# A graph network on one core: the columns of its dense count matrices, from one window's own to one per node

## The chip, the cores and the metric

The kernel runs on one core of one Trainium2 chip. The metric is device time in microseconds for one execution, as the median of repeated runs.

## The reference

Four graph layers run one after the other on 6250 nodes of 128 features and 100,000 edges. The edges are sorted by `dst`; `src` is random. `dst` is the square of a uniform number times 6250, so low nodes have many edges and high nodes few.

```python
x = _layernorm(x + tensor_product_layer(x, src, dst, edge_attr_4, edge_attr_10))
x = _layernorm(x + gated_gru_layer(x, edge_index))       # messages * sigmoid(att)
x = _layernorm(x + two_sort_convolutions(x, edge_index)) # 4 first edges of a node
x = _layernorm(x + four_sage_layers(x, edge_index))
# in a sage layer
msg = z[src]
agg = segment_sum(msg, dst, num_segments=n_nodes)
mean = agg / maximum(cnt, 1.0)
return mean @ Wl.T + bl + z @ Wr.T
```

Hidden widths of the sage layers are 256 after the first three and 128 after the last; inputs of the second to fourth are 256 wide.

## The kernel before, in words

**Tiles and groups.** 128 edges are a tile (784 tiles) and four tiles a group (196 groups). Everywhere but in the dense part a group is worked off thus: POOL issues an indirect gather of 128 rows for each tile, DVE makes one-hots of the edges' nodes relative to the group's base node, PE multiplies rows by one-hots into 128 columns of PSUM, and DVE adds those into the SBUF aggregate at the base, which it loads into a register.

**The dense part.** The first tiles, whose nodes have the most edges, are not gathered in the gate pass and the sage passes ("hot" tiles; the rest are "cold"). Instead a matrix holds, for each of 49 blocks of 128 source nodes and each column of the destination, how many edges run between them (f16, in HBM, `dense`). A pass then reads 49 blocks of counts and of the node table in order ("dense steps") and PE multiplies table by counts. Consecutive hot tiles, at most 16, form a window; a window has columns of its own, 16 to 34 of them, whose first stands for the window's first node. A node that two windows share has a column in each. The start nodes lie in `hot_bases`, and where a column's sum is used, the code loads starts into registers and takes the windows one by one.

**Building the counts** (`LateBuild`, L2409 to L2491). For a tile DVE makes a one-hot of `src % 128` (L2441, four tiles at once) and one of the key (block, column) (L2447), PE multiplies them into PSUM, `pass_counts_ps` (L2461), up to 49 x 30 f32. At a window's last tile ACT copies PSUM to the stage buffer in SBUF as f16 (L2479). When 256 columns are full, SP stores the stage to `dense` (L2490). There is one PSUM region: a window's first product waits for the eviction of the window before. The part that the gate pass needs (376 tiles, 1792 columns) is built within the tensor pass, in its 190 first turns (a turn is a group), with one stage buffer; the late part (160 tiles, 78 windows) in the two sort phases.

**The tensor pass** (layer one) gathers all 784 tiles (L1124) and runs hidden products (L1172), weights (L1182) and sums (L1203) on PE.

**The gate pass** (`gate_pass`, L1266 to L1578; 102 cold groups, 406 gathers) takes the dense columns in two halves of 896. `at_dense_columns` (L1409) computes each window's destination term at its start node. A dense step is an ACT sigmoid (L1349), a DVE product with the counts (L1503) and PE products (L1424); there is one for each of the first 98 groups. The halves are added window by window (L1547).

**The sage passes** (`sage_pass`, L1585 to L1870). The two in the middle are "wide" (256 table columns, 2304 dense columns, 420 hot tiles, 91 cold groups, 362 gathers), the first and last "slim" (128, 3840, 536, 62, 246). Dense steps (L1725) are spread over the cold groups, SP streams their operands. `spread_counts` (L1821) copies the inverse counts window by window into dense columns, L1833 scales the sums by them, `add_dense` (L1847) adds each window into the aggregate; it loads up to 24 starts at once (L1760). The node's own term is L1707, group sums are L1751.

Of the kernel before, what the change touches and what calls it, by code (L numbers as in the profile page):

```python
# [24 lines left out]
PE_E = mybir.EngineType.PE  # L25

# [29 lines left out]
def room_for(first, end):  # L56

    nodes = expected_node(end) - expected_node(first)
    return 2 * math.ceil((nodes * (1 + 3.5 / math.sqrt(P * (end - first))) + 1) / 2)


def hot_windows():


    cuts, widths = [0], []
    for bound, whole in BOUNDS:
        first, room = cuts[-1], bound - sum(widths)
        best = {first: (0, [])}
        for end in range(first + 1, first + room):
            ways = [(best[a][0] + room_for(a, end), len(best[a][1]), best[a][1] + [end])  # L70
                    for a in range(max(first, end - MOST_TILES), end) if a in best and room_for(a, end) <= NARROW]
            if min(ways)[0] > room:
                break
            best[end] = min(ways, key=lambda way: way[0] + way[1])[::2]
        end = max(t for t in best if t % whole == 0)
        ends = best[end][1]
        fitted = [room_for(a, b) for a, b in zip([first] + ends, ends)]
        while sum(fitted) < room:
            fitted[fitted.index(min(fitted))] += 2
        cuts, widths = cuts + ends, widths + fitted  # L80
    return cuts, widths


NARROW = 30
MOST_TILES = 16
GATE_COLS = 1792
WIDE_COLS = 2304
SLIM_COLS = 3840
STAGE_COLS = 256
BOUNDS = [(at, GROUP_TILES if at in (GATE_COLS, WIDE_COLS, SLIM_COLS) else 1)  # L90
          for at in sorted({GATE_COLS // 2, WIDE_COLS // 2, SLIM_COLS // 2, *range(STAGE_COLS, SLIM_COLS + 1, STAGE_COLS)})]
HOT_CUTS, WIDTHS = hot_windows()
EDGES = list(itertools.accumulate(WIDTHS, initial=0))
DENSE_WINDOWS = len(WIDTHS)
DENSE_TILES = HOT_CUTS[-1]
GATE_WINDOWS = EDGES.index(GATE_COLS)
HOT_TILES = HOT_CUTS[GATE_WINDOWS]
HOT_GROUPS = HOT_TILES // GROUP_TILES
COLD_GROUPS = GROUPS - HOT_GROUPS
KEYS = BLOCKS * max(WIDTHS)  # L100
SUPERS = 2
SUPER_COLS = GATE_COLS // SUPERS
STEPS = SUPERS * BLOCKS
GATE_STREAM = 4
ADD_WINDOWS = 8
# [17 lines left out]
def windows_between(first_col, end_col):  # L123
    return list(range(EDGES.index(first_col), EDGES.index(end_col)))


def hot_tiles_of(columns):
    return HOT_CUTS[EDGES.index(columns)]

# [2965 lines left out]
```

## Time and profile before

| What | us |
|---|---|
| Runs before: median of 3 (lowest, highest) | 4715.51 (4713.63, 4729.36) |
| The profiled execution's own time | 4711.36 |
| Its span | 4709.5 |
| PE busy, POOL busy, DVE busy, ACT busy | 3546.9, 3057.2, 2819.4, 1252.7 |

The phases follow one another: preparation and first table to 94 us, tensor pass to 1175, gate pass from 1273 to 1895, sort phases from 2021 to 2585, then four sage passes from 2665, 3165, 3735 and 4285, the output last. No engine is busy for the whole span, so what a part is worth is read from the phase that it lies in. A view by windows of time gives each engine's busy time there; the waits tell what ended an engine's idle time; the timeline shows single instructions. Timeline rows give start, time, engine, line, operation and in brackets the idle time before it. A line view's row gives count, busy time, mean ns of one and the idle time before the group's instructions.

### The profile page before, as it was taken

What the parts mean: (1) busy time and instruction counts of PE and PEld (TensorE: products, weight loads), DVE (VectorE), ACT (ScalarE), POOL (GpSimd) and SP (SyncE); (2) the same over time, 40 slices, a digit from 0 to 9 for tenths busy, and PEclk for the clock granted to TensorE, in tenths of its full rate; (3) what the DMA queues carried; (4) which work ended last, traced back from release to release, by engine and by line L of the source; (5) the groups of instructions that cost most, each with busy time, mean ns of one, the idle gap of its engine ahead of it and who ended that gap; (6) DMA issues with size and microseconds to landing.
All of it is one profiled execution on the core that took longest, in us unless ns stands there. A gap on an engine that the chain in (4) does not pass through costs nothing. (4 is left out here: it accounts for less than half of the span.)

```text
span 4709.5 us, 73302 instructions
## 1 busy us (share of the span) xinstructions
PE 3546.9 (75%) x24179; PEld 2502.4 (53%) x24180; DVE 2819.4 (60%) x8637; ACT 1252.7 (27%) x2796; POOL 3057.2 (65%) x2999
## 2 busy tenths in 40 slices
PE   3788887777777777556445598679998699967894
PEld 2666666666644544333222464447766576755552
DVE  4898888887466666677677534354444535354334
ACT  2333344444244343334333200020000200002112
POOL 3777777777277576367477575537776577746663
PEclk7899999998899898765555799889999899988996
DMA  5222333334233343033333586438886488856872
GB/s 194 66 69 64 94 93 93 91 92 140 73 99 100 81 102 78 18 83 105 90 102 82 197 261 199 149 116 267 265 256 198 164 262 264 261 179 216 247 225 81
DMA packets 432943, 684.60 MB, mean 145 GB/s; under 512 B 66971, under 2 KB 306501, under 8 KB 431801
## 3 DMA queue, kind: packets, MB, share of 16 engines
q1 hardware_dynamic: 311992, 385.14, 25.5%
q0 software_dynamic: 120576, 294.77, 22.7%
q8 instruction: 198, 3.24, 0.3%
q14 instruction: 177, 1.44, 0.1%
HBM read 577.20 MB, written 102.45 MB: 144 GB/s over the span
## 5 line engine op out<-in xcount | busy, mean ns | idle before, releaser
L1664 POOL DMA_INDIRECT pass_rows<-table_sage,src_idx x1216 | 1175.8, 967 | 476.7 <-issue 350.3
L1124 POOL DMA_INDIRECT pass_rows<-table_tensor,src_idx x784 | 834.4, 1064 | 246.8 <-issue 236.8
L1725 PE MATMUL pass_dense_ps<-x 128*128 128x512 f16 (+3 forms) x3528 | 605.8, 327 | 31.8 <-DMA x<-table_sage 30.7
L1333 POOL DMA_INDIRECT pass_rows<-table_gate,src_idx x406 | 433.7, 1068 | 202.3 <-issue 118.2
L1725 PE MATMUL pass_dense_ps<-rb 128*128 128x512 f16 (+1 forms) x2352 | 508.7, 373 | 27.4 <-DMA rb<-table_sage 25.2
L2528 POOL DMA_INDIRECT sort_rows<-table_sort,slot_idx x392 | 396.5, 1012 | 182.1 <-issue 162.3
L1751 PE MATMUL pass_sums_ps<-pass_hot,pass_rows 128*128 128x128 bf16 x5856 | 394.7, 224 | 85.9 <-issue 85.9
L1725 PEld LDWEIGHTS pass_dense_ps<-x 128*128 128x128 bf16 x3528 | 314.4, 98 | 266.6 <-DMA x<-table_sage 31.9
L1751 PEld LDWEIGHTS pass_sums_ps<-pass_hot,pass_rows 128*128 128x128 bf16 x5856 | 367.3, 101 | 108.2 <-issue 92.3
L1786 DVE TENSOR_TENSOR pass_scaled_sums<-pass_sums_ps,rc 128x128 f32<-128x128 f32 x364 | 88.9, 285 | 479.4 <-PE pass_sums_ps L1751 471.6
L1725 PEld LDWEIGHTS pass_dense_ps<-rb 128*128 128x128 bf16 x2352 | 229.2, 100 | 263.6 <-DMA rb<-table_sage 26.3
L1154 ACT ACTIVATE pass_y_ea<-pass_rows,rd 128x128 f32<-128x128 f32 x784 | 250.0, 391 | 405.8 <-DMA pass_rows<-table_tensor,src_idx 405.7
L2461 PE MATMUL sort_counts_ps<-sort_hot_key,sort_hot_low 128*128 128x512 bf16 (+4 forms) x502 | 190.8, 519 | 194.2 <-DVE sort_hot_key L2447 150.5
L1203 PE MATMUL pass_sums_ps<-pass_hot,pass_prod_a 128*128 128x128 f32 x1568 | 234.9, 297 | 131.8 <-DVE pass_prod_b L1015 131.0
L1203 PEld LDWEIGHTS pass_sums_ps<-pass_hot,pass_prod_a 128*128 128x128 f32 x1568 | 209.7, 206 | 186.7 <-issue 177.8
L2461 PE MATMUL pass_counts_ps<-rc 128*128 128x512 bf16 (+8 forms) x1039 | 238.1, 355 | 88.5 <-ACT re L2479 88.5
L1424 PE MATMUL pass_dense_ps<-pass_weighted,rd 128*128 128x512 f32 (+1 forms) x392 | 191.8, 616 | 113.2 <-DVE pass_weighted L1503 110.7
L1786 DVE TENSOR_TENSOR rb<-pass_sums_ps,rc 128x128 f32<-128x128 f32 x124 | 36.0, 290 | 350.6 <-PE pass_sums_ps L1751 334.1
L1203 PE MATMUL pass_sums_ps<-pass_hot,pass_prod_b 128*128 128x128 f32 x1568 | 228.9, 294 | 0.0
L1182 PE MATMUL pass_weight_ps<-fc,pass_hidden 100*128 100x128 f32 x1576 | 221.5, 286 | 1.5 <-ACT pass_hidden L1141 1.0
L1203 PEld LDWEIGHTS pass_sums_ps<-pass_hot,pass_prod_b 128*128 128x128 f32 x1568 | 212.8, 211 | 0.0
L2461 PEld LDWEIGHTS sort_counts_ps<-sort_hot_key,sort_hot_low 128*128 128x128 bf16 x502 | 52.9, 124 | 293.8 <-issue 192.5
(351 smaller groups left out, 6758.1 us busy)
## 6 DMA issues: line engine op xcount, KB each, us to landing
rb<-dense SPq DMA_DIRECT2D x196, 480.0 KB
x<-dense SPq DMA_DIRECT2D x196, 288.0 KB
x<-table_sage SPq DMA_DIRECT2D x196, 192.0 KB
dense<-re SPq DMA_DIRECT2D x11, 3136.0 KB, 13.7
pass_counts<-dense SPq DMA_DIRECT2D x98, 224.0 KB
pass_rows<-table_sage,src_idx POOLq DMA_INDIRECT x1216
rb<-table_sage SPq DMA_DIRECT2D x196, 96.0 KB
table_sage<-x SPq DMA_DIRECT2D x24, 768.0 KB
```

The lines of the kernel that those rows point to most:

```text
L1124: nc.gpsimd.indirect_dma_start(rows[:, h, t, :], None, table, bass.IndirectOffsetOnAxis(ap=idx[:, at:at + 1], axis=0)).then_inc(gathered[h ...
L1154: ins = nc.scalar.activation(y_ea0[:, r, t, :], rows[:, h, t, :], ACT.Copy, scale=cols(extra["edge_attr"], (q * GROUP_TILES + t) * 4, 1))
L1182: ins = nc.tensor.matmul(weight_ps[:, r, t * P:(t + 1) * P], hidden[:, r, t * P:(t + 1) * P], extra["w_fc2"], start=True, stop=True)
L1203: ins = nc.tensor.matmul(sums[:, r, a * WIN:(a + 1) * WIN], prod[:, r, t, :], hot[:, r, t, :], start=(t == 0), stop=(t == GROUP_TILES - 1))
L1333: nc.gpsimd.indirect_dma_start(rows[:, h, t, :], None, table, bass.IndirectOffsetOnAxis(ap=idx[:, at:at + 1], axis=0)).then_inc(gathered[h ...
L1424: ins = nc.tensor.matmul(dense_ps[:, at:to], messages[:, k, 0:P], weighted[:, n % 2, at:to], start=(b == 0), stop=(b == BLOCKS - 1))
L1664: nc.gpsimd.indirect_dma_start(rows[:, h, t, :], None, table, bass.IndirectOffsetOnAxis(ap=idx[:, at:at + 1], axis=0)).then_inc(gathered[h ...
L1725: ins = nc.tensor.matmul(dense_ps[:, at:to], table_ring[:, k, from_table:from_table + P], counts_ring[:, k, at - first:to - first], start= ...
L1751: ins = nc.tensor.matmul(sums[:, r, a * P:(a + 1) * P], rows[:, h, t, at:at + P], hot[:, r, t, :], start=(t == 0 and part == 0), stop=(t = ...
L1786: ins = nc.vector.tensor_tensor(scaled_sums[:, a, :], sums[:, r, a * P:(a + 1) * P], cols(inv_count, start, WIN), ALU.mult)
L2461: ins = self.nc.tensor.matmul(self.counts[:, at:at + wide], self.hot_low[:, (t // G) % 2, t % G, :], self.hot_key[:, r, at:at + wide], sta ...
L2528: nc.gpsimd.indirect_dma_start(rows[:, b, j, :], None, table, bass.IndirectOffsetOnAxis(ap=slot_idx[:, at:at + 1], axis=0)).then_inc(gathe ...
```

## The change

A dense column now is a node. The near matrix covers nodes 0 to 2047 and the hot tiles 0 to 443 (126 windows), the late one nodes 1980 to 3163 and tiles 444 to 551 (54 windows); they are two tensors in HBM. Where a window begins within its stage is only known from the data, so preparation computes a table `offsets` with ten doubling steps of a running minimum, and PE, ACT and SP load an offset into a register where they need it. A window that begins in a column that the one before also has takes that column's counts over by a product with the identity (L2503); stages that nothing has written yet are cleared first (L2528). Stores are 256 columns wide, each waits for the one before, and they overlap.

| | before | now |
|---|---|---|
| Near: tiles, columns, windows, stores | 376, 1792, 69, 7 | 444, 2048, 126, 11 |
| Late: tiles, windows, stores | 160, 78, 8 | 108, 54, 7 |
| Gate pass: cold groups, gathers | 102, 406 | 85, 338 |
| Gate pass: dense steps x columns | 98 x 896 | 98 x 1024 |
| Wide sage pass: gathers; steps x columns | 362; 98 x 1152 | 338; 98 x 1024 |
| Slim sage pass: gathers; steps x columns | 246; 98 x 1920 | 230; 49 x 2048 and 49 x 1184 |

In the gate pass 15 groups now hold two dense steps and 26 take a second hot group's slot operands. The diff, cut to its core:

```diff
+            offset = self.position(PE_E, HOT_CUTS[w], STAGE_COLS - 1)
+            self.nc.tensor.matmul(self.counts[:, 0:BLOCKS], self.same,
+                                  stage[:, :, bass.ds(offset, 1)].rearrange("p b d -> p (b d)"),
+                                  start=False, stop=False, skip_group_check=True)
...
-        self.nc.scalar.activation(self.staged(q % n)[:, :, at:at + wide],
-                                  self.counts[:, 0:BLOCKS * wide].rearrange("p (b d) -> p b d", d=wide),
+        stage = self.staged(q % n)
+        if w == first and self.empties(q):
+            self.nc.scalar.activation(stage, self.iota[:, 0:STAGE_COLS].unsqueeze(1).broadcast_to([P, BLOCKS, STAGE_COLS]),
+                                      ACT.Copy, scale=0.0).then_inc(self.emptied, 1)
+            act.wait_ge(self.emptied, sum(map(self.empties, range(self.part[0], q + 1))))
+        if w > self.first:
+            act.wait_ge(self.evicted, w - self.first)
+        at = self.position(ACT_E, HOT_CUTS[w], STAGE_COLS - wide) if w > first else 0
+        self.nc.scalar.activation(stage[:, :, bass.ds(at, wide)],
+                                  self.counts[:, 0:BLOCKS * wide].rearrange("p (d b) -> p b d", b=BLOCKS),
                                   ACT.Copy).then_inc(self.evicted, 1)
...
+        if q > 0:
+            sp.wait_ge(self.stored[(q - 1) % n], 16 * ((q - 1) // n + 1))
+        at = self.position(SP_E, HOT_CUTS[first] + 1, self.most) if q > 0 else 0
+        sp.dma_start(self.dense[:, :, bass.ds(at, STAGE_COLS)].rearrange("b p d -> p b d"),
+                     self.staged(q % n)).then_inc(self.stored[q % n], 16)
...
+                for at in range(0, SUPER_COLS, 512):
+                    ins = nc.tensor.matmul(gate_ps[:, at:at + 512], extra["w_dst"], cols(x, u * SUPER_COLS + at, 512),
+                                           start=True, stop=True)
...
+                into = agg[:, u * SUPER_COLS:(u + 1) * SUPER_COLS]
+                nc.vector.tensor_tensor(into, into, kept if u == 0 else dense_ps[:, 0:SUPER_COLS], ALU.add).then_inc(dense_added, 1)
...
-            def spread_counts(u, part):
...
+                    nc.vector.tensor_tensor(kept[:, at:at + nodes], dense_ps[:, at:at + nodes],
+                                            inv_count[:, node:node + nodes], ALU.mult).then_inc(dense_kept, 1)
```

PE in the tensor pass, in two late turns (`L2461` is the count product before, `L2508` the same now). Before:

```order
L1182 MATMUL pass_weight_ps<-fc,pass_hidden 128x128 x4
L1172 MATMUL pass_hidden_ps<-pass_edge_terms,fc_stack 100x512
L2461 MATMUL pass_counts_ps<-rc 128x512 x2
L2461 MATMUL pass_counts_ps<-rc 128x446
L2461 MATMUL pass_counts_ps<-rc 128x512 x2
L2461 MATMUL pass_counts_ps<-rc 128x348
L1203 MATMUL pass_sums_ps<-pass_hot,pass_prod_a 128x128 x4
L1203 MATMUL pass_sums_ps<-pass_hot,pass_prod_b 128x128 x4
L1182 MATMUL pass_weight_ps<-fc,pass_hidden 128x128 x4
L1172 MATMUL pass_hidden_ps<-pass_edge_terms,fc_stack 100x512
```

Now:

```order
L1218 MATMUL pass_sums_ps<-pass_hot,pass_prod_a 128x128 x4
L1218 MATMUL pass_sums_ps<-pass_hot,rd 128x128 x4
L1197 MATMUL pass_weight_ps<-fc,pass_hidden 128x128 x4
L1187 MATMUL pass_hidden_ps<-pass_edge_terms,fc_stack 100x512
L2508 MATMUL pass_counts_ps<-rc 128x512 x2
L2508 MATMUL pass_counts_ps<-rc 128x152
L2461 TENSOR_LOAD offsets
L2503 ISA
L2503 MATMUL pass_counts_ps<-re,rc 128x49
L2508 MATMUL pass_counts_ps<-rc 128x512 x2
L2508 MATMUL pass_counts_ps<-rc 128x152
L1218 MATMUL pass_sums_ps<-pass_hot,pass_prod_a 128x128 x4
```

Two tiles a turn stay, with shorter products, but a turn now also has a window's end: an offset is loaded, and the product `counts<-re,rc` stands ahead of the new window's own.

ACT in the tensor pass (`L2479` the eviction before, `L2534` now), near the end of the windows. Before:

```order
L2479 ACTIVATE re<-pass_counts_ps 128x49x28
L1141 ACTIVATE pass_hidden<-pass_hidden_ps 100x512
L1154 ACTIVATE pass_y_ea<-pass_rows,rd 128x128 x4
L2479 ACTIVATE re<-pass_counts_ps 128x49x28
L1141 ACTIVATE pass_hidden<-pass_hidden_ps 100x512
L1154 ACTIVATE pass_y_ea<-pass_rows,rd 128x128 x4
L1141 ACTIVATE pass_hidden<-pass_hidden_ps 100x512
L1154 ACTIVATE pass_y_ea<-pass_rows,rd 128x128 x4
```

Now:

```order
L2461 TENSOR_LOAD offsets
L2534 ISA
L2534 ACTIVATE re<-pass_counts_ps 128x49x24
L1156 ACTIVATE pass_hidden<-pass_hidden_ps 100x512
L1169 ACTIVATE pass_y_ea<-pass_rows,rd 128x128 x4
L2461 TENSOR_LOAD offsets
L2534 ISA
L2534 ACTIVATE re<-pass_counts_ps 128x49x24
L2528 ACTIVATE re<-rc 128x12544
L2534 ACTIVATE re<-pass_counts_ps 128x49x24
```

Where there was an eviction every turn or two there is one every turn, behind the load of its offset, and the last stage is cleared (`L2528`) ahead of its only window.

DVE at the end of the last sage pass. Before, one of three rounds of window adds:

```order
L1806 SCALAR_TENSOR_TENSOR ra<-pass_own_ps,sage_decoded_b,ra 128x128
L1760 TENSOR_LOAD hot_bases
L1847 ISA
L1847 TENSOR_TENSOR ra<-ra,pass_kept 128x26
L1847 ISA
L1847 TENSOR_TENSOR ra<-ra,pass_kept 128x26
L1847 ISA
L1847 TENSOR_TENSOR ra<-ra,pass_kept 128x26
L1847 ISA
L1847 TENSOR_TENSOR ra<-ra,pass_kept 128x26
```

Now, in the whole of it:

```order
L1807 TENSOR_TENSOR ra<-ra,rb 128x128
L1820 SCALAR_TENSOR_TENSOR ra<-pass_own_ps,sage_decoded_b,ra 128x128
L1835 TENSOR_TENSOR pass_kept<-pass_dense_ps,rc 128x1184
L1844 TENSOR_TENSOR ra<-ra,pass_kept 128x1184
L1789 TENSOR_TENSOR pass_hot<-sage_iota_half,rb 128x512
L1774 TENSOR_LOAD bases
L1800 ISA
L1800 TENSOR_TENSOR rb<-pass_sums_ps,rc 128x128
```

The rounds of adds at loaded starts are gone; one add over 1184 columns (2048 in the first half) follows the scaling at once.

## Rows read from the trace of the kernel before

**Rows 1.** The windows view: from:to, us, busy us by engine, granted clock, DMA share, GB/s.

```profile
94.00:1175.00 1081.00, 853.70 (x5898) 695.38 (x5899) 918.55 (x2606) 432.25 (x1046) 834.37 (x784) 0.93 0.33 90
...
1273.00:1575.00 302.00, 224.06 (x1276) 154.10 (x1276) 189.56 (x547) 118.23 (x296) 226.61 (x212) 0.90 0.39 99
...
2665.00:3036.00 371.00, 324.36 (x2174) 195.34 (x2174) 133.14 (x516) 17.99 (x49) 240.20 (x246) 0.93 0.74 230
...
3165.00:3630.00 465.00, 449.72 (x4236) 320.44 (x4236) 195.69 (x732) 43.01 (x98) 348.18 (x362) 0.99 0.82 258
```

**Rows 2.** The lines view by shape, 94 to 1175 us (the tensor pass).

```profile
L1124 POOL DMA_INDIRECT pass_rows<-table_tensor,src_idx x784 | 834.4, 1064 | 246.8 <-issue 236.8 <-PE pass_sums_ps L1203 5.7 <-POOLq L201 4.3
...
L2447 DVE TENSOR_SCALAR rc<-rc 128x1470 bf16<-128x1470 f16 x138 | 83.1, 630 | 0.0
...
L2479 ACT ACTIVATE re<-pass_counts_ps 128x1470 f16<-128x1470 f32 x20 | 27.9, 1394 | 31.6 <-PE pass_counts_ps L2461 28.7 <-DMA dense<-re 2.9
```

**Rows 3.** The waits view, same stretch: waiter <- releaser: total, times, longest.

```profile
PE pass_counts_ps L2461 <- ACT re L2479: 88.5, 41, 10.3
...
ACT re L2479 <- DMA dense<-re: 21.1, 4, 9.6
...
POOL pass_rows L1124 <- PE pass_sums_ps L1203: 5.7, 6, 2.6
```

**Rows 4.** The timeline of PE, 1082 to 1100 us.

```profile
1082.85 1.33 PE L2461 MATMUL pass_counts_ps<-rc 128*128 128x512 bf16 x3 [7.00 <-ACT re L2479]
1083.97 1.92 PE L1203 MATMUL pass_sums_ps<-pass_hot,pass_prod_a 128*128 128x128 f32 x8
...
1088.85 1.33 PE L2461 MATMUL pass_counts_ps<-rc 128*128 128x512 bf16 x6
1090.02 1.05 PE L1203 MATMUL pass_sums_ps<-pass_hot,pass_prod_a 128*128 128x128 f32 x8
...
1092.16 1.13 PE L1182 MATMUL pass_weight_ps<-fc,pass_hidden 100*128 100x128 f32 x8 [0.20 <-ACT pass_hidden L1141]
...
1093.35 1.33 PE L2461 MATMUL pass_counts_ps<-rc 128*128 128x512 bf16 x6
```

**Rows 5.** The lines view, 1273 to 1895 us (the gate pass).

```profile
L1333 POOL DMA_INDIRECT pass_rows<-table_gate,src_idx x406 | 433.7, 1068 | 202.3 <-issue 118.2 <-PE pass_sums_ps L1452 44.5 <-POOLq L201 39.6
...
L1424 PE MATMUL pass_dense_ps<-pass_weighted,rd 128*128 128x512 f32 x196 | 118.1, 686 | 113.2 <-DVE pass_weighted L1503 110.7
...
L1503 DVE TENSOR_TENSOR pass_weighted<-pass_counts,pass_gate_ps 128x896 f32<-128x896 f16 x98 | 105.8, 1079 | 32.1 <-issue 16.4 <-ACT pass_gate_ps L1349 15.6
```

**Rows 6.** The timeline of PE and of DVE in the gate pass.

```profile
1577.66 5.73 PE L1409 MATMUL pass_gate_ps<-x,wdst 128*128 x26
...
1886.63 2.38 DVE L1547 TENSOR_TENSOR ra<-ra,pass_dense_ps 128x26 f32 x8 [1.84 <-issue]
```

**Rows 7.** The timeline of PE, 3400 to 3412 us (a wide sage pass).

```profile
3401.47 3.09 PE L1725 MATMUL pass_dense_ps<-x 128*128 128x512 f16 x18
3404.39 1.06 PE L1707 MATMUL pass_own_ps<-pass_z_block,sage_wr 128*128 128x128 f32 x8
3405.29 1.50 PE L1751 MATMUL pass_sums_ps<-pass_hot,pass_rows 128*128 128x128 bf16 x24
3406.63 3.09 PE L1725 MATMUL pass_dense_ps<-x 128*128 128x512 f16 x18
```

**Rows 8.** The waits view, 3165 to 3630 us (wide), then 4300 to 4630 (slim).

```profile
POOL pass_rows L1664 <- issue: 106.3, 348, 0.5
...
POOL pass_rows L1664 <- PE pass_sums_ps L1751: 9.0, 13, 2.6
...
POOL pass_rows L1664 <- PE pass_sums_ps L1751: 35.6, 12, 8.6
```

**Rows 9.** The timeline of DVE, 4620 to 4660 us (the end of the last sage pass).

```profile
4642.50 7.45 DVE L1847 TENSOR_TENSOR ra<-ra,pass_kept 128x24 f32 x24 [5.18 <-issue]
```

**Rows 10.** The lines view of DVE, 0 to 30 us (preparation).

```profile
L1961 DVE TENSOR_TENSOR prep_place<-prep_dst,prep_hot_base 128x536 f32<-128x536 int32 x1 | 0.7, 706 | 0.0
```

More of the change, by code:

```diff
@@ L58, in room_for @@
     nodes = expected_node(end) - expected_node(first)
[L59 to L81, printed above, removed]
@@ L1093, in _ @@
             sp.wait_ge(extra["split_stored"], 16 * SPLIT)
-            stages = list(range(len(build.runs)))
+            stages = list(range(*build.part))
             for i in range(ITERS + 1):
@@ L1836, in add_dense @@
[L1836 to L1849 removed]
+                    at = a * most_cols
@@ L1970, in _ @@
[L1970 to L1974 removed]
+            nc.vector.tensor_scalar(block_part, src_idx[:, 0:DENSE_TILES], 7, None, ALU.arith_shift_right)
@@ new lines, in _ @@
+            for _, _, node, _, _, runs in SHARES:
+                for a, _ in runs:
+                    at = HOT_CUTS[a]
+                    nc.vector.tensor_scalar(offsets[:, at + 1:at + 2], based[0:1, at:at + 1], float(-node), None, ALU.add)
+            nc.vector.tensor_copy(low, low_part)
+            nc.vector.tensor_copy(block_f, block_part)
+            nc.vector.tensor_scalar(under, place, -1.0, -1.0, ALU.mult, ALU.add)
+            after(nc.vector.tensor_tensor(over, place, hot_width, ALU.subtract))
@@ new lines, in _ @@
+            nc.vector.tensor_scalar(near, rel[:, 0:DENSE_TILES], WIN - 0.5, None, ALU.is_le)
+            nc.vector.tensor_scalar(close, rel[:, 0:DENSE_TILES], HOT_WIN - 0.5, None, ALU.is_le)
+            nc.vector.reduce_max(most_rel[:], rel[:, 0:TILES], mybir.AxisListType.X)
+            nc.vector.scalar_tensor_tensor(keyed, place, float(BLOCKS), block_f, ALU.mult, ALU.add)
+            after(nc.vector.tensor_tensor(least_of[0][:], over, under, ALU.max))
+            for first, end, _, node, _, _ in SHARES:
+                ins = nc.vector.scalar_tensor_tensor(least_of[1][:, first:end], dst[:, first:end], float(-node),
+                                                     least_of[0][:, first:end], ALU.add, ALU.max)
@@ L1991, in _ @@
         def _(pe):
-            pe.wait_ge(step, 6)
+            pe.wait_ge(step, 2)
             for src, ps in ((passed, count_ps), (stepped, base_ps)):
@@ L2424, in __init__, with empties, run_of, position @@
         self.low_made, self.key_made, self.counted, self.evicted = (s.sem(n) for n in ("low_made", "key_made", "counted", "evicted"))
+        self.emptied = s.sem("emptied")
+    def empties(self, q):
+        return q < len(self.stages) or q == len(self.runs) - 1
+    def run_of(self, w):
+        return next(q for q, (first, end) in enumerate(self.runs) if first <= w < end)
+    def position(self, engine, at, most):
+        _, values = self.nc.values_load_multi_w_load_instructions(
+            self.offsets[0:1, at:at + 1], engines=[engine], min_val=0, max_val=most,
+            skip_runtime_bounds_check_because="a window begins within the one before it")
+        return values[0]
     def turns(self, turn, count):
@@ L2473, in evict @@
         w, n = w + self.first, len(self.stages)
-        q, (first, _) = next((q, run) for q, run in enumerate(self.runs) if w < run[1])
-        at, wide, stored = EDGES[w] - EDGES[first], WIDTHS[w], self.stored_before[q % n] + q // n
-        if w == first and stored > 0:
-            act.wait_ge(self.stored[q % n], 16 * stored)
+        q = self.run_of(w)
+        first, end, wide = *self.runs[q], WIDTHS[w]
+        if w == first and q >= n:
+            act.wait_ge(self.stored[q % n], 16 * (q // n))
```

523 lines of the change are left out of this document (277 added, 246 removed).

## The prediction

> **What bounds the kernel now.** I read the windows view first, since the four engines' busy times over the whole span all leave gaps and none names a bound [rows 1]. Its stretches say what each phase hangs on; then the lines view of a stretch gives prices, and the waits view tells which engine is late.
>
> In the tensor pass PE is busy 854 us and POOL 834 us of 1081 [rows 1], but POOL's row has 247 us of idle time of which 237 is plain issue: (834.4 + 236.8)/784 = 1.366 us a gather, end to end [rows 2]. It waited for PE only 5.7 us in all [rows 3]. So POOL is the bound, 5.46 us a turn of four gathers, and PE runs close behind. PE waited 88.5 us for evictions, 41 times [rows 3], and the gathers, some groups ahead, hid it.
>
> In the gate pass (1273 to 1895) no engine is full; a group takes 5.5 us on average (560 us of steady work by 102 groups), against 4 x (433.7 + 118.2)/406 = 5.44 us that POOL needs [rows 5]. POOL waits 44.5 us for PE there.
>
> In a wide sage pass PE is busy 449.7 of 465 us at a granted clock of 0.99, and DMA moves 258 GB/s [rows 1]. POOL's 348.2 busy and 106.3 issue make 454.5 us, 1.256 us a gather, and it waited 9.0 us for PE [rows 1, 8]. PE, POOL and DMA stand nearly level. In a slim pass POOL waits for PE 35.6 us [rows 8], PE is the bound, and at the end DVE holds all up with window adds.
>
> **Preparation, +17 us.** It is one chain on DVE. A 128-row operation over 536 columns takes 0.71 us [rows 10]. Ten doubling steps of a partial copy and a minimum, 0.9 us each with the wait between, are 9; about 18 offset operations of some 0.2 are 4; the other additions less what goes are about 4. It is all ahead of the first table, so it counts in full; bounds 0 (if loads cover it) and 22.
>
> **Tensor pass, +65 us.** POOL's work stays. PE gains an offset load and a product of 49 columns at 125 window ends, and 125 evictions stand where 68 stood. I take the last 76 turns, where the hot tiles' windows are shortest: 70 of the windows end there, 40 of them with the next window's first tile in the same turn, and 7 stages. A turn on PE was 4.50 us (1088.85 to 1093.35) with two tiles, 2842 columns, in 1.17 us of it, and 0.20 us of waiting [rows 4]. There are now 2.34 tiles a turn, of 1176 columns: 1.13. So 4.50 - 0.20 - 0.04 = 4.26, times 76 = 324. A window end: 0.3 for load and product, times 70 = 21. A hand-over in one turn leaves PE idle for the eviction (1.39 us for 1470 columns [rows 2], so 1.12 for 1176) and, newly, ACT's load of its offset and two semaphores, 1.75 in all, times 40 = 70. That makes 415, just POOL's 76 x 5.46 = 415: the cover that hid PE's waits is used up. What comes on top is no longer hidden. A store keeps the only stage buffer, and the eviction after it waits up to 9.6 us [rows 3], PE 7.0 us, after which PE's turn from 1083.97 to 1088.85 took 4.88 where from 1090.02 to 1093.35 it took 3.33 [rows 4]: 7 to 8 and 1.5, so 9.5 a stage. Seven stages are 66, the last clear (12,544 columns at 0.95 ns by the eviction's row less its start, about 11) makes 77. Less the 7 to 12 us that POOL runs ahead, +65. Bounds: 0, if POOL's lead covers the waits as it did before (5.7 us of waiting at four stage waits), and +120, if each hand-over costs a microsecond more than I take.
>
> The eviction now reads PSUM with a step of 49 words. No row has that; the nearest is the contiguous 1394 ns [rows 2], and I take it, for a single f32 is read an element at a time in either case. The Trainium skill, Advanced Engine Details and Errata, section Memory Cachelines, has PSUM in lines of 8 bytes and says that every two consecutive elements should be contiguous, which speaks against this change. No row here shows a stepped read; if it doubled the eviction, the sum would be some 110 us higher.
>
> **Between and sorts, -2 us.** A small block and clears add 4 to 6 us; sort phases keep their gathers, and the build there has 324 products where it had 502. It lay under POOL.
>
> **Gate pass, -45 us.** Destination terms at window starts took 5.73 us for 26 products with register loads [rows 6], with PE's whole queue behind them; two products of 512 replace 35 or so. That is 10 at the start and 12 in the middle. At the end, four rounds of window adds with 1.84 us of register loads before 2.4 of adds [rows 6] lie behind one another: -20. Between: 17 groups fewer, 98 steps 1/7 wider. All of the removed gathers would be 68 x 1.36 = -92; all of the widening in series (PE's four products of at most 0.69 us, 2.5 in all, DVE 1.08 [rows 5], and as much for ACT's sigmoid over the same columns: 4.6/7 x 98) +64. Doubled steps in 15 groups, second slot operands in 26: I take -3, as the two nearly cancel. Bounds -110 and +20.
>
> **Sage passes, -220 us.** Wide: a dense step is 2.92 us for 6912 columns, a group's sums 1.34 us [rows 7], 0.42 ns a column. 98 steps lose 768 columns: -31; six groups fewer: -8. PE falls from 450 to 411. POOL has 338 gathers x 1.256 = 424.5. So POOL becomes the bound, -40 a pass with the tail of adds: 474 us from first gather to end becomes 434. DMA: 119.4 MB become 111.5, at the 258 GB/s of rows 1 432 us, still level. Two passes, -80. Slim: PE's columns go from 3 x 98 x 1920 to 3 x 49 x 3232, -89,376 x 0.417 = -37, four groups -3, so 324 [rows 1] becomes 284, and POOL's 230 gathers, at 1.28 us (the wide pass's 1.256, and 2% for its start), 294 us, are the bound. The tail goes: rounds of 5.2 us of loads and 7.5 of adds [rows 9], PE behind them. 371 us [rows 1] and 370 us (4285 to 4655) become 303 and 298: -68 and -72. Bounds: -20 and -50 a pass for wide, -45 and -75 for slim.
>
> **The sum.** 17 + 65 - 2 - 45 - 220 = -185 on the profiled execution's 4711.4: 4526. The median of the runs is 4 us above that execution, so I say 4528.
>
> **The rivals.**
> *The hand-overs stay hidden* (0.15). For it: POOL lost just 5.7 us to PE at 41 hand-overs [rows 3]. Against it: my own level sum. Then 4528 - 65 = 4463.
> *DMA takes the place of POOL in the sage passes* (0.15). Three things stand level there, and the counts' rows are no longer at even addresses: a row of the near matrix is 5708 B, where all was a multiple of 256 B. By the rate of rows 1, 258 GB/s, and 4% more traffic, a wide pass takes 448 in place of 425, a slim one 12 more: +70, so 4598. The Trainium skill, DMA: Bandwidth & Descriptors, section How a descriptor splits into AXI transactions, has a descriptor that starts off a 256 B boundary fetch the bytes below it too; a row of 2048 B would need nine transactions as 2304 B did. The traces so far have even rows alone.
> *The gate pass gives nothing* (0.08). The chain of a doubled step, not the gathers, sets the group's time: +64 of widening less some of the groups. Then 4528 + 45 + 15 = 4588.
> *Slower: the stepped read of PSUM* (0.05). The evictions lie on the chain PE, ACT, PE, so 125 of them pay in full once PE is the bound. Decides from 2.4 times the price on: 125 x 1.12 x 1.4 = 196 us, more than the whole gain. At three times, +280: 4808. For it: an eviction by 49 words takes one word from each line. Against it: no row. At twice the price it is 4640, faster still (0.02).
> That the change doesn't do what it says, where an offset that falls out wrong sends many edges to the slow path for stray edges, I leave within these: each pass already has that path and it costs the same when empty.
>
> **The numbers.** The forecast's own case has 0.55, and its terms' bounds give 4470 to 4590. With the first two rivals the range is 4455 to 4625, which leaves out the two cases of the stepped read and both far tails. A measurement here can tell 0.3%, 14 us. Faster by more: all but the last rival and a mixture of the unlucky bounds, 0.93; within 0.02, slower 0.05.
>
> **What would show it.** Tensor pass: it ends near 1255 in place of 1175, POOL waits for PE some 60 us there, most at stages, and the eviction of 1176 columns takes 1.1 us; if 2 or more, the stepped read costs. Gate pass: 338 gathers, PE's long runs of destination products and DVE's last rounds gone, about 577 us long. Wide sage: 338 gathers, POOL idle for nothing but issue, PE busy about 410, the pass 434 us; if POOL waits for PE and PE for DMA, the second rival. Slim: 230 gathers, about 300 us, no add after the last group. The forecast is wrong if the tensor pass grows by nothing or by over 120 us, or if a sage pass is bound by anything but its gathers.

## The result: 3.5 times as long

The changed kernel takes 16746.08 us (median of 4, 16736.5 to 16753.44) where the kernel before takes 4720.66 (median of 4, 4713.63 to 4729.36): a ratio of 3.547, interval 3.540 to 3.554. The forecast was 4528. From the page of the changed kernel: the span, the busy times, the groups of gathers and the stores of the counts (count, KB each, us to landing). Landing is the time from a store's issue until it has arrived. The groups of L2098 have no counterpart in [rows 2, 5]:

```profile
span 16751.6 us, 138868 instructions
...
PE 6002.6 (36%) x38254; PEld 4252.7 (25%) x38255; DVE 5094.9 (30%) x14676; ACT 1585.9 (9%) x3642; POOL 6317.3 (38%) x6439
...
L2098 POOL DMA_INDIRECT pass_far_rows<-table_sage,pass_far_idx x2760 | 2608.3, 945 | 6047.3 <-DMA pass_far_idx<-in_src 5313.5
...
L2098 POOL DMA_INDIRECT pass_far_rows<-table_gate,pass_far_idx x636 | 603.6, 949 | 2080.4 <-DMA pass_far_idx<-in_src 1908.0
L1682 POOL DMA_INDIRECT pass_rows<-table_sage,src_idx x1136 | 1110.4, 977 | 367.0 <-issue 341.1
...
L2098 POOL DMA_INDIRECT pass_far_rows<-table_tensor,pass_far_idx x192 | 181.0, 943 | 637.0 <-DMA pass_far_edge_in<-in_edge_in 590.0
...
dense<-re SPq DMA_DIRECT2D x14, 3136.0 KB, 27.0
```

POOL now issues 2760, 636 and 192 gathers from L2098, and the trace of before has none of these: the line is in `far_pass`, the loops for stray edges that stand behind each of the six passes over the edges. They run if one flag is set: an edge lies 128 nodes or more past its group's base, or an edge of a hot tile has no column in the count matrices. Then they run whole: 48 groups of four gathers after the tensor pass, and after each of the other passes 48 and all hot groups (111, or 138 in the slim passes). The first and last gathers of each phase in the timeline of POOL give this (in brackets the length):

| Phase | before, us | changed, us |
|---|---|---|
| Tensor pass, 784 gathers | 94.8 to 1171.7 | 114.8 to 1427.0 |
| Loops behind it | none | 1450.7 to 2245.1 (794) |
| Gate pass | 1273.1 to 1869.5 | 2341.8 to 2843.0 |
| Loops behind it | none | 2866.3 to 5526.9 (2661) |
| Slim, wide, wide, slim: gathers | 360, 463, 464, 344 | 297, 433, 432, 294 |
| Loops behind them | none | 2136, 2162, 2171, 2137 |

The loops are 12,061 us in all. Here is a piece of them behind the first wide pass, in the timeline of all engines:

```profile
9399.65 0.95 POOL L2098 DMA_INDIRECT pass_far_rows<-table_sage,pass_far_idx  x1 [0.30 <-issue]
...
9402.83 2.74 PE L2152 MATMUL pass_far_sums_ps<-pass_far_hot,pass_far_rows 128*128 128x128 bf16 x24 [10.93 <-DMA pass_far_rows<-table_sage,pass_far_idx]
9405.72 0.49 DVE L2222 TENSOR_TENSOR pass_far_scaled_sums<-pass_far_sums_ps,rc 128x128 f32<-128x128 f32 x2 [10.01 <-PE pass_far_sums_ps L2152]
...
9407.19 0.34 SPq L2087 DMA_DIRECT2D pass_far_idx<-in_src  x1
...
9409.62 0.94 POOL L2098 DMA_INDIRECT pass_far_rows<-table_sage,pass_far_idx  x1 [9.02 <-DMA pass_far_idx<-in_src]
```

A group's indices are loaded only when the group before has been added (the DMA at 9407.19, 2.4 us before POOL's gather). Then come four gathers, their landing, 24 products, two scalings and the adds, one after another: 13.7 us a group, of which PE waits 10.93. The windows view shows two such stretches, each behind the pass that it follows; the columns are those of [rows 1]:

```profile
2340.00:2860.00 520.00, 397.79 (x2230) 244.55 (x2230) 383.09 (x1108) 229.85 (x540) 365.88 (x338) 0.94 0.42 106
2860.00:5540.00 2680.00, 937.25 (x2896) 470.65 (x2896) 548.92 (x1754) 181.48 (x636) 603.55 (x636) 0.50 0.08 16
...
8893.00:9340.00 447.00, 418.90 (x3608) 277.27 (x3608) 171.30 (x535) 42.27 (x97) 330.10 (x338) 0.98 0.80 251
9340.00:11515.00 2175.00, 435.94 (x3816) 394.00 (x3816) 428.39 (x1280) 0.00 (x0) 600.93 (x636) 0.52 0.21 58
```

Over the loops PE is busy 35% and 20% of the time and POOL 23% and 28%, where POOL was busy 70% and 74% in the passes, and TensorE's granted clock is 0.50 and 0.52, its level of 1.2 GHz, where it was 0.94 and 0.98 in the passes.

### The profile page after: what moved, and what is told of

It is laid out like the page before. It is cut to its first block and busy times, and to the rows that moved or that the text cites. A ratio compares the mean times of both kernels' runs of the same rounds, so it can differ in the third digit from the quotient of the medians.

```text
span 16751.6 us, 138868 instructions
## 1 busy us (share of the span) xinstructions
PE 6002.6 (36%) x38254; PEld 4252.7 (25%) x38255; DVE 5094.9 (30%) x14676; ACT 1585.9 (9%) x3642; POOL 6317.3 (38%) x6439
## 5 line engine op out<-in xcount | busy, mean ns | idle before, releaser
L2098 POOL DMA_INDIRECT pass_far_rows<-table_sage,pass_far_idx x2760 | 2608.3, 945 | 6047.3 <-DMA pass_far_idx<-in_src 5313.5
L2152 PE MATMUL pass_far_sums_ps<-pass_far_hot,pass_far_rows 128*128 128x128 bf16 x12096 | 1415.8, 313 | 7230.0 <-DMA pass_far_rows<-table_sage,pass_far_idx 7230.0
L2152 PEld LDWEIGHTS pass_far_sums_ps<-pass_far_hot,pass_far_rows 128*128 128x128 bf16 x12096 | 1233.7, 147 | 7412.0 <-DMA pass_far_rows<-table_sage,pass_far_idx 7412.0
L2098 POOL DMA_INDIRECT pass_far_rows<-table_gate,pass_far_idx x636 | 603.6, 949 | 2080.4 <-DMA pass_far_idx<-in_src 1908.0
L2155 PE MATMUL pass_far_sums_ps<-pass_far_hot_sig,pass_far_rows 128*128 128x128 f32 x1272 | 506.7, 502 | 1620.0 <-DVE pass_far_hot_sig L2200 1620.0
L2184 DVE TENSOR_TENSOR pass_far_match<-iota,pass_far_moved 128x512 f32<-128x512 f32 x897 | 621.0, 692 | 30.8
L2187 DVE TENSOR_TENSOR pass_far_hot<-pass_far_match,pass_far_past 128x512 bf16<-128x512 f32 (+1 forms) x897 | 620.8, 692 | 30.5
L1741 PE MATMUL pass_dense_ps<-x 128*128 128x512 f16 x2352 | 541.4, 383 | 31.3 <-DMA x<-table_sage 30.9
L1741 PE MATMUL pass_dense_ps<-rb 128*128 128x512 f16 x2058 | 424.8, 361 | 24.4 <-DMA rb<-table_sage 23.9
L1360 POOL DMA_INDIRECT pass_rows<-table_gate,src_idx x338 | 365.9, 1082 | 174.2 <-issue 94.1
L2098 POOL DMA_INDIRECT pass_far_rows<-table_tensor,pass_far_idx x192 | 181.0, 943 | 637.0 <-DMA pass_far_edge_in<-in_edge_in 590.0
L2156 PE MATMUL pass_far_slot_ps<-pass_far_hot,pass_far_slot_in 128*9 128x128 f32 x1272 | 379.6, 402 | 0.0
```

Source lines behind the costliest of these rows:

```text
L1360: nc.gpsimd.indirect_dma_start(rows[:, h, t, :], None, table, bass.IndirectOffsetOnAxis(ap=idx[:, at:at + 1], axis=0)).then_inc(gathered[h ...
L1741: ins = nc.tensor.matmul(dense_ps[:, a * most_cols + at:a * most_cols + to], table_ring[:, k, from_table:from_table + P], counts_ring[:, k ...
L2098: nc.gpsimd.indirect_dma_start(rows[:, t, :], None, table, bass.IndirectOffsetOnAxis(ap=idx[:, t:t + 1], axis=0)).then_inc(far.gathered, 16)
L2152: ins = nc.tensor.matmul(sums[a][:, 0:WIN], rows[:, t, at:at + P], hot[:, t, :], start=(first and part == 0), stop=(last and part == PARTS ...
L2155: nc.tensor.matmul(sums[0][:, 0:WIN], rows[:, t, 0:P], hot_sig[:, t, :], start=first, stop=last)
L2156: ins = nc.tensor.matmul(slot_ps[0:SLOT_ROWS, 0:WIN], slot_in[:, t, :], hot[:, t, :], start=first, stop=last)
```

## Why the loops run

The table of window bases can be worked out from the reference's own `dst`. The late matrix begins at node 1980 (`LATE_FROM`), and its windows are laid side by side from there: a window may not begin beyond the end of the one before. Its first tile, 444, begins at node 2001. A window is 26 columns wide here, and the next one begins in its last column, which the window's own edges can't use. The first window (tiles 444, 445) has columns up to node 2004 of its own, while its edges go to 2019. The second has them up to 2029 (edges to 2037), the third up to 2054 (edges to 2055), and the fourth has caught up. So 298 of 100,000 edges, in tiles 444, 445, 447 and 449, have no column and are left to the loops. By the text of the kernel one such edge opens all of these; whether it is so, the runs below ask.

## The experiments

There are fourteen runs. A ratio is to the kernel before on the same chip. Four runs (free_stage, split_stores, gate_narrow, even_rows) fell on a chip on which the kernel before takes 5245.71 us in place of 4711; they are compared with it and with one another alone. The kernels of even_stores, shift32, shift1, both free_stage runs and gate_narrow leave counts out or put them in other columns; they serve to time a part.

**mended.**

```diff
-NEAR_NODES, LATE_FROM, LATE_TO = 2048, 1980, 3164
+NEAR_NODES, LATE_FROM, LATE_TO = 2048, 1996, 3164
```

> The changed kernel with one number changed: the late matrix starts at node 1996 in place of 1980, so that its windows, laid side by side from there, reach the 298 edges of tiles 444, 445, 447 and 449 that they passed over. Theory A (those edges alone set the flag that opens the loops for stray edges in all six passes): the loops' 12,017 us go, by the gaps between the gathers of the changed kernel's trace against those of before, and the window rounds at the pass ends with them: 4685 us, 4655 to 4720. Rival B (the loops are opened by something else, say a node far from its group's base): still 16,700. Rival C (the far work is there because offsets are wrong in general): fewer loops, but not none.

Measured: 4594.61 us (5 runs), ratio 0.9752, 0.9728 to 0.9775. A second time, beside the later runs:

> The mended kernel a second time, beside the runs below on one chip, since the four runs before these fell on a chip where all kernels take longer (the kernel before 5246 us in place of 4711). Ratio to the kernel before as measured first: 0.975.

4597.15 us (4 runs), ratio 0.9748, 0.9729 to 0.9767. No gather of L2098 is left. Theory A holds: of the 12,151 us between the two kernels 12,061 are the loops. The number is 60 us below the lowest of its range. The tensor pass is 28 us shorter than in the changed kernel's profile, with its stores landing in 24.6 us in place of 27.0. The rest is put down to the ends of the passes, which the gaps that I subtracted hold; no run separates it.

**three_missed**, the same with 1994.

> The changed kernel with the late matrix from node 1994: 3 edges of tile 445 are passed over in place of 298. Theory A (one flag opens every loop, whatever the number): 16,740, as the changed kernel, within 30 us. Rival D (the cost goes with the edges or with the groups that hold them): under 4900.

Measured: 16700.7 us (1 run), 39 us below the 16,740. Its loops take 12,035 us, so three edges cost what 298 did, and rival D is out; 32 us of the difference lie in the tensor pass (1280.4 us of gathers in place of 1312.2; mended has 1284.4).

**before_flag**, on the kernel before.

```diff
-            nc.vector.tensor_scalar(far.any[:], top[:], float(WIN), None, ALU.is_ge)
+            nc.vector.tensor_scalar(far.any[:], top[:], 0.0, None, ALU.is_ge)
```

> The kernel before, with the flag for stray edges set although no edge is stray: every loop runs and adds zeros. By the changed kernel's durations of a group (16.55 us in the tensor pass, 16.73 gate, 11.5 slim, 13.6 wide) and its own counts (48, 142, 182 twice, 153 twice): 794 + 2376 + 4186 + 4162 = 11,520 more, 16,240 us. If the loops' price were a matter of the changed kernel's tables or of its PSUM or SBUF layout, it would be clearly less.

Measured: 16260.37 us (1 run), 20 us from the sum. The loops were as dear in the kernel before; on these data they had never run.

**even_stores.** The rest of the forecast, which mended lets one read, was wrong in the tensor pass above all. The waits view of mended there (113 to 1398 us):

```profile
POOL pass_rows L1139 <- PE pass_sums_ps L1218: 233.2, 46, 34.3
...
PE pass_counts_ps L2508 <- ACT re L2534: 213.1, 69, 21.7
...
ACT re L2534 <- DMA dense<-re: 171.9, 9, 25.2
...
ACT re L2528 <- DMA dense<-re: 23.4, 1, 23.4
```

Beside [rows 3]: POOL waits 233 us for PE where it waited 5.7. ACT waits 195 us for stores, ten times, where it waited 21, four times.

```diff
-    return sum(WIDTHS[w] - 1 for w in SHARES[share][4]) + STAGE_COLS
+    return -(-max(sum(WIDTHS[w] - 1 for w in SHARES[share][4]) + STAGE_COLS, STAGE_COLS * len(SHARES[share][5])) // P) * P
...
-        at = self.position(SP_E, HOT_CUTS[first] + 1, self.most) if q > 0 else 0
-        sp.dma_start(self.dense[:, :, bass.ds(at, STAGE_COLS)].rearrange("b p d -> p b d"),
+        at = q * STAGE_COLS
+        sp.dma_start(self.dense[:, :, at:at + STAGE_COLS].rearrange("b p d -> p b d"),
```

> On the mended kernel: the rows of both dense tensors are padded to multiples of 256 bytes and the stores go to fixed multiples of 256 columns, so the counts lie in other columns than the nodes' and the aggregates differ from the reference; the number and size of the stores and all waits stay. Theory E (a store of 512-byte rows at odd addresses takes twice as long, 27.0 against 13.7 us, and PE and POOL wait for it): landing 13.7 to 15 us, ACT's waits for stores in the tensor pass from 230 us to 80 to 100, the pass 130 us shorter, the whole 4555 +- 30. Rival F (the doubling is due to gathers and streams beside it, or to each store waiting for the one before): landing stays 25 to 28, time within 15 us of the mended kernel.

Measured: 4466.31 us (4 runs), ratio 0.9472, 0.9449 to 0.9496; 128 us under mended. The waits view, same stretch, and then the page's line of the stores (count, KB, landing in us):

```profile
POOL pass_rows L1139 <- PE pass_sums_ps L1218: 116.9, 43, 23.2
...
ACT re L2534 <- DMA dense<-re: 86.8, 9, 12.8
...
ACT re L2528 <- DMA dense<-re: 13.3, 1, 13.3
```

```profile
dense<-re SPq DMA_DIRECT2D x14, 3136.0 KB, 13.5
```

Mended's page has 24.6 there, the changed kernel's 27.0, before 13.7. The gathers of the tensor pass take 1178.0 us in place of 1284.4. Theory E holds and F is out; the whole lies below the 4525 to 4585 that I gave, since I had counted from the 4685 expected of mended, while the drop, 128 us, is the 130 expected.

**shift32 and shift1.** On even_stores; `SHIFT` is 32 or 1.

```diff
-        at = q * STAGE_COLS
+        at = q * STAGE_COLS - SHIFT * (q > 0)
```

> even_stores with every store but the first begun 32 columns, 64 bytes, before the multiple of 256 columns; counts in other columns than the nodes' as there. If rows of 512 bytes must begin at a multiple of 512 bytes to be fast: landing 22 to 27 us. If 64 bytes do: 13.5 to 15. I expect the latter at 0.6.

> The same with 1 column, 2 bytes: landing 22 to 27 us as in the mended kernel, whose offsets are arbitrary, if the place of a row's start is all that made its stores slow. If it stays at 13.5, the cause is another that even_stores took away with it, as the register in the store's address.

Measured: shift32 4466.28 us, landing 14.3; shift1 4563.09 us, landing 24.3 (1 run each). Rows of 512 bytes that begin 64 bytes off are nearly as fast as even ones (14.3 against 13.5). Begun 2 bytes off they make a store 10 us longer, although its place is a constant and no register is in the address. Mended_again is another 34 us longer than shift1, though its stores land in 24.4; its stores in the sort phases from the second stage buffer land in 35.4, shift1's in 27.4. Why arbitrary columns cost this much more than 2 bytes stays open, and nothing between 2 and 64 bytes was tried.

**even_rows.** The rows padded, the stores at the data's columns.

```diff
+    return -(-(sum(WIDTHS[w] - 1 for w in SHARES[share][4]) + STAGE_COLS) // P) * P
```

> On the mended kernel, whole computation: the rows of the dense tensors are padded to a multiple of 256 bytes; the stores still begin at the data's own columns. If the price of a store is by where its rows begin, little changes, since most offsets (109, 304, 501, 699, ...) are off a 256-byte boundary whatever the pitch: landing 22 to 25 us, time within 15 us of 4595. If the pitch was the cause: landing 14 and 4490. The sage passes read rows that now begin at even addresses; by the POOL bound their gathers stay at 298 and 430 us.

Measured: 5141.64 us (4 runs), ratio 0.9808, 0.9787 to 0.983; landing 25.2. The pitch (the distance of two rows) was not the cause. The sage gathers took 339.1 and 511.2 us, in free_stage beside it, with its odd rows, 339.2 and 512.1: odd rows cost a reader nothing here.

**split_stores and halves_in_turn.** In split_stores each store goes out as two halves (cut to the core):

```diff
+        cut = STAGE_COLS if self.half is None else STAGE_COLS // 2
+        sp.dma_start(self.dense[:, :, bass.ds(at, cut)].rearrange("b p d -> p b d"),
+                     self.staged(q % n)[:, :, 0:cut]).then_inc(self.stored[q % n], 16)
+        if self.half is not None:
+            sp.dma_start(self.dense[:, :, bass.ds(at + cut, cut)].rearrange("b p d -> p b d"),
+                         self.staged(q % n)[:, :, cut:STAGE_COLS]).then_inc(self.half, 16)
```

> On the mended kernel, whole computation: each store of the tensor pass goes out as two, columns 0 to 127 and 128 to 255 of the stage; the first eviction of the next stage waits for the first half alone, the window that may pass column 128 for the second. Theory G with a price by bytes: a stage wait falls from 24 us to 12 or 13, ten of them are 110 to 120: 4480 +- 30. Rival J (the price is by row, and rows of 256 bytes cost as much each as those of 512): the wait stays at 20 to 25 and nothing is gained: 4580 to 4620.

Measured: 5211.55 us (8 runs), ratio 0.9934, 0.9912 to 0.9956: 70 us above even_rows, and by its ratio worse than both the rival and the theory had it. Two halves in flight landed after 24.6 us each, and the last clear now waited 45.1 us, so the run can't tell the two apart. In halves_in_turn one half follows the other:

> The mended kernel with the stores of the tensor pass in halves, as split_stores, but the second half is issued only when the first has landed. In split_stores the two halves of 1568 KB ran side by side and landed together after 24.6 us. Theory G, price by bytes: the first half lands in 12 to 13 us alone, the ten stage waits fall by 11 us each, 110 us less than the mended kernel beside it. Rival J (rows of 256 bytes cost as much as rows of 512): a half takes 20 us or more, under 30 us gained.

Measured: 4637.27 us (6 runs), ratio 0.9845, 0.9832 to 0.9859, 40 us above mended. The page's line:

```profile
dense<-re SPq DMA_DIRECT2D x22, 1568.0 KB, 22.1
```

A half of 1568 KB takes 22.1 us where the whole of 3136 KB takes 24.4 in mended_again beside it. Rival J holds: at odd places the price is nearly by row. It gained nothing, since the last clear now waits for two halves, 42.1 us.

**free_stage, and again.**

```diff
-        if w == first and q >= n:
+        if w == first and q >= n and self.source is None:
...
-                     self.staged(q % n)).then_inc(self.stored[q % n], 16)
+                     self.staged(q % n) if self.source is None else self.source).then_inc(self.stored[q % n], 16)
```

> On the mended kernel: in the tensor pass the same 11 stores, of the same size and to the same places, are read from a constant tile in place of the stage buffer, and the first eviction of a stage no longer waits for a store; so the near counts in memory are not the edge counts. Theory G (what a store costs is the wait for the one stage buffer, 171.9 + 23.4 us on ACT, straight through PE to POOL): the waits go, the pass falls from 1284 us of gathers to 1090 to 1115, the whole to 4420 +- 25. Rival H (the slow stores take memory bandwidth or queue time from the gathers): the pass stays above 1180, the whole above 4490.

Measured: 4988.62 us (4 runs), ratio 0.9502, 0.9476 to 0.9528; gathers 1267.8 us, with no mended kernel beside it (the gathers of even_rows took 1415.0 there). It doesn't tell what is left, so:

> The kernel of free_stage, on a chip where the kernel before takes 4711 us if it falls so (free_stage fell on the slower one and has no mended kernel beside it). Theory G: without any wait for a store the gathers of the tensor pass take 1284 - 195 = 1090 us, POOL's wait for PE falls from 230 us to under 40, the whole is 4400 +- 20. Rival M (the 125 hand-overs between PE and ACT cost the pass as much as the stores): gathers take 1130 to 1180 us, the whole 4440 to 4500.

Measured: 4437.05 us (4 runs), ratio 0.9425, 0.9411 to 0.944. Gathers 1126.0 us; from the waits view:

```profile
PE pass_counts_ps L2509 <- ACT re L2535: 128.4, 69, 11.1
...
POOL pass_rows L1140 <- PE pass_sums_ps L1219: 62.2, 32, 12.4
```

Both numbers lie just under Rival M's ranges and some 36 us above what Theory G gave. Rival H, that the stores take bandwidth or queue time from the gathers, is out too: it had the pass above 1180 and the whole above 4490. Of the 207 us by which the gathers had grown in mended, the waits for stores were 158. The other 49 stay: they are the hand-overs and the two clears (with whatever the traffic of the stores adds). POOL waits 62 us with no store in the way.

**gate_narrow.** `SOME` is 896, as wide as the steps before the change. The sigmoid is one of six places that use it.

```diff
-                nc.scalar.activation(gate_ps[:, 0:SUPER_COLS], at_dense[:], ACT.Sigmoid,
+                nc.scalar.activation(gate_ps[:, 0:SOME], at_dense[:, 0:SOME], ACT.Sigmoid,
```

> On the mended kernel: the gate pass works on 896 of the 1024 columns of each half (reads, sigmoid, product, matmuls and add); the last 128 columns of each half are left out. Theory K (the gate pass goes with its gathers and group operations; wider steps lie beside them): gathers from 502 us to 490 to 502, the whole down by under 12 us. Rival L (the widening is in series, up to 64 us as the prediction's bound had it): 440 to 465 us, the whole down by 40 to 64.

Measured: gathers 518.4 us, in the three kernels beside it 524.5, 526.9 and 530.7; the whole 5166.19 us, ratio 0.9873, 0.9844 to 0.9902. The gathers speak for Theory K and against Rival L's 440 to 465 us. The 6 to 12 us themselves are no more than a spread: the gate pass of full width took 501.5 to 513.1 us over the eight mended kernels on the other chips. The whole has no like kernel beside it to be compared with.

**even_runs.** The whole computation with stores at multiples of 32 columns, which needs a table of rounded starts and, at a stage's first window (cut to the core):

```diff
+                at = self.position(ACT_E, DENSE_TILES + len(RUNS) + self.run_from + q, STAGE_COLS - EVEN)
+                self.nc.scalar.activation(stage[:, :, 0:EVEN], self.staged((q - 1) % n)[:, :, bass.ds(at, EVEN)],
+                                          ACT.Copy).then_inc(self.emptied, 1)
```

> The mended kernel, whole computation, with stores that begin at a multiple of 32 columns (64 bytes) and rows padded to 256 bytes: a stage begins with a copy of 32 columns out of the stage before, so that it can start up to 31 columns early. The stages hold less: 13 stores where there were 11. Twelve stage waits of 13.7 us and a copy of 1.5 us are 182, where ten of 24.4 were 244: the tensor pass 1220 us of gathers, sorts 10 us shorter, the whole 4525 +- 25, ratio to the kernel before 0.960. If the copy or the two more stages cost more than this, 4560 to 4600.

Measured: 4523.27 us (5 runs), ratio 0.9605, 0.9592 to 0.9618. Gathers of the tensor pass 1224.0 us, landing 13.5. It is 4% faster than the kernel before and 1.5% faster than mended, as expected (4525).

## Why the prediction was wrong

**The step that failed** is the one sentence about stray edges: that the path "costs the same when empty", so that I left it "within these". The path was not empty. I had read in the change that bases are a running minimum held at or above a start node, and had never put the reference's `dst` through it; that takes no chip. Nor was the path priced: before_flag shows that 11,550 us stood behind the flag in the kernel before too. The rival that a change doesn't do what it says had no chance and no price, and it was the case that came: 12,061 us of loops. No term of the sum bears on it.

The terms can be read from mended, which differs in one number. By the first gathers of the phases, from one profile each (mended_again has 9 us more in the gate pass and within 2 us the same in the tensor pass):

| Term | forecast | mended, profiled |
|---|---|---|
| Preparation and first table | +17 | +18.5 |
| Tensor pass, to the gate's first gather | +65 | +215 |
| Gate pass, to the sort's first gather | -45 | -102 |
| Sort phases, to the first sage gather | -2 | +37 |
| Sage passes, to the end | -220 | -285 |
| Sum | -185 | -116 |

*Preparation.* Right.

*Tensor pass.* The gathers went from 1076.9 to 1284.4 us. The reading was right that PE's cover was used up, so that stage waits reach POOL. Two terms were mis-sized. The first is the stage wait. A store lands in 24.6 us and not 13.7, and ACT waits 19.5 us a stage on average, up to 25.2; with even stores it is 10.0. That is 106 us by even_stores, a cost for which my list had no line, though the change's text shows stores at arbitrary columns. I saw odd rows as a danger to the sage passes that read them, and not to the stores. With even stores the ten stage waits cost 52 us (1178.0 against 1126.0 in free_stage_again), less than the 66 that I had for seven. The second is what I took as level with POOL, at nothing: 49 us by free_stage_again, of which the last clear, which I had, is 11. The hand-overs themselves were sized right: in that run PE waits for ACT 40 times and 68 us in the last 76 turns of the build, against my 40 and 70. What failed is the level sum, 415 against 415, which left them no price. The stepped eviction cost little; ACT's lines in mended, then one of the kernel before:

```profile
L2534 ACT ACTIVATE re<-pass_counts_ps 128x1176 f32 x27 | 32.9, 1217 | 89.4 <-PE pass_counts_ps L2508 89.4
...
L2528 ACT ACTIVATE re<-rc 128x12544 f16<-128x12544 f16 x2 | 21.3, 10656 | 23.4 <-DMA dense<-re 23.4
...
L2534 ACT ACTIVATE re<-pass_counts_ps 128x1470 f32 x8 | 11.3, 1408 | 34.8 <-PE pass_counts_ps L2508 34.8
```

```profile
L2479 ACT ACTIVATE re<-pass_counts_ps 128x1176 f16<-128x1176 f32 x4 | 4.6, 1151 | 9.2 <-PE pass_counts_ps L2461 9.2
```

For 1176 elements it is 1217 ns against 1151, for 1470 elements 1408 against 1394 of [rows 2]. That is far from the 2.4 times that the rival needed, and it is out. (Its middle case was summed wrongly: twice the price is 125 x 1.12 = 140 us more, 4668 and not 4640. No row priced ACT's load of its offset or PE's window end either.) The Trainium skill, Advanced Engine Details and Errata, section Memory Cachelines, which I weighed, wants every two consecutive elements of PSUM contiguous; ACT's reads here, which have none contiguous, take 1 to 6% more in these lines. The clear is 10.7 us, as taken.

*Gate pass.* I let the widening nearly cancel the groups, at -3, though my own prices, -92 and +64, leave -28. The time between first and last gather fell from 596.4 to 501.6 us with the gathers from 406 to 338: 1.469 and 1.484 us each. If the shorter destination terms gave their 22 there, the groups gave some 73. Gate_narrow shows nothing like 64 us for the wider steps, 12 at most. My bound of -110, and not the middle, was the nearer number. POOL's row shows why: it waits for PE 41.2 us, no more than before. The end of the pass, behind the last gather, gave 7 us in place of 20.

```profile
L1360 POOL DMA_INDIRECT pass_rows<-table_gate,src_idx x338 | 366.3, 1084 | 174.0 <-issue 94.1 <-PE pass_sums_ps L1474 41.2 <-POOLq L215 38.7
...
L1529 DVE TENSOR_TENSOR pass_weighted<-pass_counts,pass_gate_ps 128x1024 f32<-128x1024 f16 x97 | 117.9, 1215 | 25.5 <-issue 18.2 <-ACT pass_gate_ps L1376 7.3
```

*Sorts.* The late stores begin at odd places as well. From the sort's first gather to the sage pass's it is 681 us in mended and 650 in even_stores, against 644 before: 31 of the 37 us are the places of the stores again, which I had left out here too.

*Sage passes.* The gathers are as forecast: slim 298.3 and 293.8 us (forecast 294), wide 430.7 and 428.7 (424.5), POOL waiting 3.0 us for PE. From mended's windows view, against [rows 1]:

```profile
2834.00:3132.00 298.00, 276.57 (x1998) 169.63 (x1997) 96.82 (x269) 17.99 (x49) 227.98 (x230) 0.97 0.82 254
3238.00:3670.00 432.00, 415.32 (x3566) 274.59 (x3567) 162.81 (x520) 42.72 (x98) 328.05 (x338) 0.99 0.83 259
```

PE is busy 415 us in the wide pass (forecast 411). What I missed is that a slim pass had not ended at 3036 us: two more rounds of window adds stood behind it, on DVE in the timeline of before:

```profile
3039.44 6.18 DVE L1847 TENSOR_TENSOR ra<-ra,pass_kept 128x24 f32 x20 [0.48 <-DVE ra L1847]
...
3052.15 7.53 DVE L1847 TENSOR_TENSOR ra<-ra,pass_kept 128x26 f32 x24 [4.79 <-issue]
...
3064.56 0.29 DVE L1793 TENSOR_TENSOR ra<-ra,rb 128x128 f32 x1
```

The last add is at 3064.6, 40 us behind the last gather, and these rounds are gone. From first gather to first gather (or the end) the slim passes gave 96 and 85 us in place of 68 and 72, and the wide ones 49 and 55 in place of 40, of which the gathers are 33 and 35. The rival that DMA takes POOL's place did not come: DMA moves 259 GB/s, and its busy share is 0.83 with odd rows as with the even ones of even_stores.

Without the stray edges the forecast of 4528 would have stood 67 us from mended's 4594.6 and inside the range, but by luck: 189 us too little were put on the tensor and sort phases, and 122 too little gained on the gate and sage passes. By my own sign, a tensor pass longer by more than 120 us, it would have been wrong even so.

## What to carry to other kernels

Where a change alters a table that decides which elements fit, put the reference's data through that table first, and price the path for those that don't: a path behind one flag costs its whole length for a few elements, here 12,035 us for three. Where a transfer's place comes from data, ask for its alignment on the writing side too, and cost each wait for the only buffer at the landing time that it will have after the change. Where one engine stands level with another, count most of each new microsecond on its chain: here 195 us of ACT's waits for stores were 158 us of the pass.

## What the runs showed of the hardware

- Stores of 6272 rows of 512 bytes from SBUF to HBM land in 13.5 to 14.3 us when rows begin at a multiple of 64 bytes (even_stores, shift32, even_runs), and in 24.3 to 27.0 when they begin 2 bytes off (shift1) or at arbitrary columns (mended, the changed kernel). Rows of 256 bytes at arbitrary columns take 22.1: the price is nearly by row. The Trainium skill, DMA: Bandwidth & Descriptors, section How a descriptor splits into AXI transactions, has a descriptor that doesn't start at a 256-byte boundary read from the boundary below, which makes three transactions of two for 512 bytes. It says this of reading. Carried over to the places that a store writes, it would have shift32 and shift1 alike; the runs have 14.3 and 24.3 us, so it doesn't describe them.
- Reads of 2048-byte rows at odd places showed no cost in the wide sage passes (430.7 us of gathers in mended, 430.1 in even_stores, DMA share 0.83 in both).
- ACT read 1470 f32 of PSUM with a step of 49 in 1408 ns, contiguously in 1394; 1176 in 1217 and 1151; 784 in 899 and 816.
- On one chip the two kernels that were also timed elsewhere took 11 and 12% longer (the kernel before 5245.71 against 4711 us, free_stage 4988.62 against 4437.05); a study needs its baseline on the same chip.
